# Two attentions of a transformer block: side work of TensorE cut into single products and pairs of transposes, spread over the key tiles

## The reference

```python
x = x + _L0_xattn_ref(_layernorm(x), ctx_1024, ctx_1024, mask, wq, bq, wk, bk, wv, bv, wo, bo)
x = x + _L0_ffn_ref(_layernorm(x), ...)    # 2 shared experts, top 2 of 8 routed experts
x = x + _L1_xattn_ref(_layernorm(x), ctx_1024, ctx_1024, key_padding_mask, Wq, bq, ...)
x = x + _L1_ffn_ref(_layernorm(x), theta, phi, theta_noise, phi_noise)

# both attentions
q, k, v = (split_heads(q), split_heads(k), split_heads(v))
score = jnp.einsum('bhqd,bhkd->bhqk', q, k) / jnp.sqrt(jnp.float32(HD))
alpha = jax.nn.softmax(score + mask, axis=-1)
context = jnp.einsum('bhqk,bhkd->bhqd', alpha, v)
return context.transpose(0, 2, 1, 3).reshape(b, -1, D) @ wo + bo

# _L1_ffn_ref
real = jnp.einsum('bti,io->bto', x, jnp.cos(theta + theta_noise))
imag = jnp.einsum('bti,io->bto', x, jnp.sin(phi + phi_noise))
return jnp.sqrt(real * real + imag * imag)
```

## Time and profile before

| | |
|---|---|
| median of 3 runs | 1262.23 us |
| the profiled execution | 1261.12 us |
| its span from first to last instruction | 1259.4 us |
| exponentials L925 on ACT | 800, 748.4 us busy |
| outputs L1834 on PE | 6400 instructions, 436.0 us busy |
| scores L1799 on PE | 6144 instructions, 316.4 us busy |
| query products L1627 | 96, 25.2 us busy |
| output projection L1861 | 128 instructions |
| wave products L1895 | 72, 19.7 us busy |

### The profile page before, as it was taken

The page is one execution under the profiler, slowest core; times in us unless marked ns, Lnnn a source line. Parts: engine busy times, 40 slices in busy tenths (PEclk is TensorE's granted clock), DMA queues, the critical chain, the costliest instruction groups (busy, mean ns, idle before and its releaser), DMA issues. The chain is left out here.

```text
span 1259.4 us, 43578 instructions
## 1 busy us (share of the span) xinstructions
PE 1164.9 (92%) x17850; PEld 581.9 (46%) x17850; DVE 720.3 (57%) x1697; ACT 1015.5 (81%) x1484; POOL 168.5 (13%) x204
## 2 busy tenths in 40 slices
PE   8888899899898999999999999988889999999897
PEld 5422232232222356667999998752222233232233
DVE  5325777767746577554666666662545444443447
ACT  3599999999999854443566666639999999999994
POOL 5111111011001030333000011032321000000000
PEclk9999999999999999999999999999999999999999
DMA  6235853643645333221343355133120010010002
GB/s 196 65 118 193 272 169 104 197 151 107 205 155 177 103 119 113 86 71 51 117 123 116 116 141 160 44 99 96 49 58 24 11 38 2 11 38 2 2 3 67
DMA packets 106305, 124.94 MB, mean 99 GB/s; under 512 B 25091, under 2 KB 89310, under 8 KB 106142
## 3 DMA queue, kind: packets, MB, share of 16 engines
q1 hardware_dynamic: 89088, 85.95, 22.1%
q0 software_dynamic: 9328, 29.37, 7.4%
q10 hardware_dynamic: 7726, 7.26, 1.9%
HBM read 70.27 MB, written 46.95 MB: 93 GB/s over the span
## 5 line engine op out<-in xcount | busy, mean ns | idle before, releaser
L925 ACT ACTIVATE prob<-banks 128x1024 f32<-128x1024 f32 x800 | 748.4, 1061 | 7.3 <-PE banks L1799 3.8
L1834 PE MATMUL banks<-prob,v 64*32 64x512 f32 x6400 | 436.0, 592 | 0.0
L1799 PE MATMUL banks<-zone,kst 52*32 52x512 f16 x6144 | 316.4, 383 | 65.7 <-ACT prob L925 58.2
L1799 PEld LDWEIGHTS banks<-zone,kst 52*32 52x32 f16 x6144 | 86.7, 89 | 444.0 <-ACT prob L925 429.5
L1834 PEld LDWEIGHTS banks<-prob,v 64*32 64x32 f32 x6400 | 117.4, 106 | 24.1 <-issue 2.2
L2503 PE MATMUL banks<-xsT_d,w 128*128 128x128 f16 x1776 | 123.6, 219 | 2.7 <-DMA w<-weight_parts 1.5
L2503 PEld LDWEIGHTS banks<-xsT_d,w 128*128 128x128 f16 x1776 | 108.6, 98 | 11.8 <-issue 8.8
L2514 PE MATMUL banks<-w,hh 128*128 128x256 f16 x592 | 107.0, 273 | 0.0
L2300 DVE TENSOR_TENSOR hl<-hid,hh 128x128 f16<-128x128 f32 x296 | 83.2, 291 | 30.9 <-ACT hh L2227 23.2
L2223 ACT ACTIVATE hid<-banks,b 128x128 f32<-128x128 f32 x222 | 74.5, 369 | 25.0 <-PE banks L2503 21.2
L2466 PE MATMUL banks<-w,hh 128*128 128x256 f16 x480 | 79.0, 273 | 2.1 <-DVE outb_d L2385 2.1
(11 more groups left out here) (302 smaller groups left out, 1367.2 us busy)
## 6 DMA issues: line engine op xcount, KB each, us to landing
weight_parts<-late SPq DMA_DIRECT2D x54, 256.0 KB, 3.9
w<-weight_parts POOLq DMA_DIRECT2D x24, 512.0 KB, 3.9
late<-in_L_ffn_W_r SPq DMA_DIRECT2D x43, 256.0 KB, 4.4
weight_parts<-more SPq DMA_DIRECT2D x26, 256.0 KB, 3.6
zone<-q_parts SPq DMA_DIRECT2D x180, 32.0 KB
slot_rows<-late POOLq DMA_DIRECT2D x14, 384.0 KB
more<-in_L_ffn_W_r SPq DMA_DIRECT2D x21, 256.0 KB, 4.2
xs_d<-slot_rows ACTq DMA_DIRECT2D x39, 128.0 KB, 2.1
```

Of the source, the lines that this page charges most:

```text
L925: nc.scalar.activation(prob[:, t % P_RING, 2 * (n % 2):2 * (n % 2) + 2, :], score[G % S_RING], ACT.Exp, scale=0.25).then_inc(exp_done, 1)
L1799: last = nc.tensor.matmul(score[G % S_RING][j:j + GROUP, a, :], kst[stack, 2 * q + n % 2, t * P + j:t * P + j + GROUP], qst[stack, u % Q_R ...
L1834: last = nc.tensor.matmul(outp[u % 2][GROUP * j:GROUP * (j + 1), a, :], v[rows, t, u % NQ, j, :], prob[rows, (u * KT + t) % P_RING, j if t ...
```

## The change

`plan` no longer takes tiles from a table. Every side work is cut into atoms: a single product of queries, output projection or waves, a pair of transposes, or one token tile's four logit products. Each group of atoms has a stretch of tiles `(t0, t1)` and is laid evenly over it, so a tile can get none, one or two atoms, which run one after the other at the tile's end. `turn_pair` replaces `turn_tokens` inside the units, `query`, `wave` and `logits` take an atom's index. The computed values, the waits in `begin`, VectorE's order and every other engine's order are the same. The tables of the last key's scores move by some tiles.

```diff
--- before.py
+++ after.py
@@ -97,11 +97,10 @@
-LAST_AT = ((4, 11, 10, 8), (5, 8, 5, 11))
+LAST_AT = ((4, 11, 11, 10), (5, 6, 6, 11))
...
-SIDES_AT = [((6, 7, 9, 10), (2, 3, 5, 6, 8, 9), (2, 4, 6, 8), (2, 4, 6)),
-            ((2, 4, 6, 7, 9, 10), (2, 4, 5, 7, 9, 10), (2, 4, 6, 8, 10, 11), (2, 4, 5, 7, 8, 10))]
-LATE_AT = ((), (7, 9), (2, 4, 6, 8), ())
...
+SIDE_PRODUCTS = DH * 3
...
@@ -1868,73 +1867,96 @@
                     last = nc.tensor.transpose(bank[:, i * P:(i + 1) * P], source[:, i, h * P:(h + 1) * P], g.ident[:])
                 last.then_inc(side_done, 1)
 
+            def turn_pair(name, c, h, k, source):
+                if k == 0:
+                    begin(name, c, h)
+                bank = side_bank(name, c, h)
+                for i in (2 * k, 2 * k + 1):
+                    last = nc.tensor.transpose(bank[:, i * P:(i + 1) * P], source[:, i, h * P:(h + 1) * P], g.ident[:])
+                if k == TPC // 2 - 1:
+                    last.then_inc(side_done, 1)
+
             def query(c, o, k):
                 if k == 0:
                     begin("query", c, o)
                     pe.wait_ge(side_free, at["turn", c, 1] + 1)
-                last = query_products(side_bank("query", c, o), o, (k,))
-                if k == DH - 1:
+                h, n = k // len(PRODUCTS), k % len(PRODUCTS)
+                a, b = PRODUCTS[n]
+                last = nc.tensor.matmul(side_bank("query", c, o), wqp[:, a, h, o * P:(o + 1) * P], xpT[:, b, h, :],
+                                        start=(k == 0), stop=(k == SIDE_PRODUCTS - 1))
+                if k == SIDE_PRODUCTS - 1:
                     last.then_inc(side_done, 1)
 
-            def logits(c):
-                bank = begin("logit", c, 0)
-                pe.wait_ge(cent_step, 4)
-                pe.wait_ge(side_free, at["xturn", c, 1] + 1)
-                for i in range(TPC):
+            def logits(c, tiles):
+                if tiles[0] == 0:
+                    begin("logit", c, 0)
+                    pe.wait_ge(cent_step, 4)
+                    pe.wait_ge(side_free, at["xturn", c, 1] + 1)
+                bank = side_bank("logit", c, 0)
+                for i in tiles:
                     for h in range(DH):
                         for a in range(PARTS):
                             last = nc.tensor.matmul(bank[:, i * 2 * E_R:(i + 1) * 2 * E_R], operands(c)[:, a, h, i * P:(i + 1) * P], centp[:, h, a, :],
                                                     start=(h == 0 and a == 0), stop=(h == DH - 1 and a == PARTS - 1))
-                last.then_inc(side_done, 1)
-
-            def wave(c, i, h):
-                if h == 0:
+                if tiles[-1] == TPC - 1:
+                    last.then_inc(side_done, 1)
+
+            def wave(c, i, k):
+                if k == 0:
                     begin("wave", c, i)
                     pe.wait_ge(side_free, at["xturn", c, 1] + 1)
-                for k, (a, b) in enumerate(PRODUCTS):
-                    last = nc.tensor.matmul(side_bank("wave", c, i), xpT[:, b, h, i * P:(i + 1) * P], g.wave[:, a, h, :],
-                                            start=(h == 0 and k == 0), stop=(h == DH - 1 and k == len(PRODUCTS) - 1))
-                if h == DH - 1:
+                h, n = k // len(PRODUCTS), k % len(PRODUCTS)
+                a, b = PRODUCTS[n]
+                last = nc.tensor.matmul(side_bank("wave", c, i), xpT[:, b, h, i * P:(i + 1) * P], g.wave[:, a, h, :],
+                                        start=(k == 0), stop=(k == SIDE_PRODUCTS - 1))
+                if k == SIDE_PRODUCTS - 1:
                     last.then_inc(side_done, 1)
 
             pe.wait_ge(shifts_loaded, 16 * 2 * NQ)
             def plan(c, q):
 
                 ahead, done = c + 1 < NC, c >= 1
-                turns = [("turn", c + 1, 0), ("turn", c + 1, 1)] if ahead else []
-                outs = [("out", c - 1, i, n, k) for i in range(DH) for n in range(2) for k in range(DH)] if done else []
-                asked = [("query", c + 1, o, k) for o in range(DH) for k in range(DH)] if ahead else []
-                back = [("xturn", c - 1, 0), ("xturn", c - 1, 1)] if done else []
-                waves = [("wave", c - 1, i, h) for i in range(TPC) for h in range(DH)] if done and not first else []
-                logit = [("logit", c - 1)] if done and first else []
-                if first:
-                    pieces = (outs[0:4], outs[4:8] + turns, asked[0:2] + back, asked[2:4] + logit)[q]
+                pairs = range(TPC // 2)
+                turns = [("turn", c + 1, h, k) for h in range(DH) for k in pairs] if ahead else []
+                outs = [[("out", c - 1, i, n, k) for n in range(2) for k in range(DH)] if done else [] for i in range(DH)]
+                asked = [[("query", c + 1, o, k) for k in range(SIDE_PRODUCTS)] if ahead else [] for o in range(DH)]
+                back = [("xturn", c - 1, h, k) for h in range(DH) for k in pairs] if done else []
+                waves = [[("wave", c - 1, i, k) for k in range(SIDE_PRODUCTS)] if done else [] for i in range(TPC)]
+                logit = [("logit", c - 1, i) for i in range(TPC)] if done else []
+                if first and done:
+                    groups = (((outs[0], 6, 10),), ((outs[1], 2, 6), (turns, 6, 10)),
+                              ((asked[0], 2, 8), (back, 8, 11)), ((asked[1], 2, 8), (logit, 8, 10)))[q]
+                elif first:
+                    groups = ((), ((turns, 7, 11),), ((asked[0], 2, 8),), ((asked[1], 2, 8),))[q]
+                elif done:
+                    groups = (((turns, 2, 5), (outs[0], 6, 10)), ((outs[1], 2, 6), (asked[0], 7, 13)),
+                              ((asked[1], 2, 6), (back, 7, 9), (waves[0], 10, 13)), ((sum(waves[1:], []), 2, 11),))[q]
                 else:
-                    pieces = (turns + outs[0:4], outs[4:8] + asked[0:2], asked[2:4] + back + waves[0:2], waves[2:8])[q]
-                times = SIDES_AT[layer][q]
-                if not first and not done:
-                    pieces, times = ([], turns, asked, [])[q], LATE_AT[q]
-                elif not done or q == 0 or (q == 2 and not first):
-                    times = times[len(times) - len(pieces):]
-                return {(LAST_AT if done else FIRST_LAST_AT)[layer][q]: ("last", c, q), **{t: piece for t, piece in zip(times, pieces)}}
+                    groups = ((), ((turns, 7, 11),), ((asked[0] + asked[1], 2, 10),), ())[q]
+                at_tile = {t: [] for t in range(KT)}
+                for atoms, t0, t1 in groups:
+                    for n, atom in enumerate(atoms):
+                        at_tile[t0 + n * (t1 - t0) // len(atoms)].append(atom)
+                at_tile[(LAST_AT if done else FIRST_LAST_AT)[layer][q]].append(("last", c, q))
+                return at_tile
 
             def side(name, c, *at_piece):
                 if name == "last":
                     last_scores(c, *at_piece)
                 if name == "turn":
-                    if at_piece[0] == 0:
+                    if at_piece == (0, 0):
                         pe.wait_ge(xn_ready, TPC * (c + 1))
-                    turn_tokens(name, c, at_piece[0], xn)
+                    turn_pair(name, c, *at_piece, xn)
                 if name == "out":
                     project_out(c, *at_piece)
                 if name == "query":
                     query(c, *at_piece)
                 if name == "xturn":
-                    if at_piece[0] == 0:
+                    if at_piece == (0, 0):
                         pe.wait_ge(on_ready, TPC * (c + 1))
-                    turn_tokens(name, c, at_piece[0], on)
+                    turn_pair(name, c, *at_piece, on)
                 if name == "logit":
-                    logits(c)
+                    logits(c, at_piece)
                 if name == "wave":
                     wave(c, *at_piece)
 
@@ -1951,8 +1973,8 @@
                         outputs((u * KT + t - 1) // KT, (t - 1) % KT)
                     if t < KT - 1 and G + 1 < UNITS * PAIRS:
                         scores(G + 1)
-                    if t in pieces:
-                        side(*pieces[t])
+                    for piece_of_work in pieces[t]:
+                        side(*piece_of_work)
             outputs(UNITS - 1, KT - 1)
 
             def hidden_ahead(a, b):
...
```

2 lines of the change are left out of this document (1 added, 1 removed).

## The result

The changed kernel takes 1271.39 us (median of five runs, 1269.51 to 1275.41) against 1262.23 us: a ratio of 1.0069 with the 95% interval 1.0054 to 1.0084. The forecast was 1263.4 us with a range of 1258.5 to 1269.5. The profiled execution took 1271.39 us, its span is 1269.6 us.

A forecast was written before the change was run, and what follows sets the result against it. The prediction took the attentions as a race between ACT's exponentials and PE, with a unit floor of about 23.0 us; its terms summed to +1.25 us, 1262.4 us profiled and a 1263.4 us median, range 1258.5 to 1269.5.

The forecast's parts named there:

- c=0 of the first attention: First attention, chunk 0: queries as single products on tiles 2 to 7 bring three units to 23.06 us each, -0.75 us.
- Rival 3: First attention, q=2, q=3: cuts waiting for loads delay the read-out, PE waits; about 1 us in eight units, 1271 us; chance 0.06.
- The waves: Second attention, q=3: six threes become nine twos, -0.15 us three times, -0.45; first wave on tiles 10 to 12 costs the same.
- the queries with their last product on tile 12: Second attention, c=1, 2, q=1: singles free on tiles 7 to 11, 0.2 us on 12, against 0.68 before; -1.0 us.
- the first chunk of the second attention: Second attention, c=0: four pieces of three become twelve products on eight tiles; -0.3 us with the turns.
- Output projection, +2.1 + 1.4: Units q=0 and q=1, both attentions: each gap lost between output products costs a 0.23 us credit; +2.1 and +1.4 us.
- Single products are free: A tile with one query product takes PE 1.74 us, leaving 0.08 us to spare against ACT's pace.
- rival 2: Tiles with pieces grow from 123 to 191; each break costs 0.23 us on the path, +15.6 us, 1278 us; chance 0.03.
- VectorE, +0.6 and +0.7: Late last scores in first attention, c=1, 2, 0.3 us each; late read-out before second attention's c=1 first wave, 0.7 us.
- Tile 12: Second attention: a single query product there was charged 0.2 us; the first wave reaching it was said to cost the same.

The follow-up runs named there:

- e1_c0_later: Changed kernel with the first attention's chunk 0 query products on tiles 5 to 9 (q=2) and 4 to 7 (q=3), not 2 to 7; 1269.97 us, ratio 1.0049.
- e2_one_cut_later: Changed kernel with one VectorE weight cut moved from the first attention's second unit to a unit of chunk 3; 1271.15 us, ratio 1.0063.
- e9_combined: Changed kernel with later chunk 0 queries, gaps between output products, waves as threes, second attention's transposes back as fours on tiles 6, 8; 1262.42 us, ratio 0.9999.
- e5_fewer_cuts: Changed kernel with 3, 4, 5 weight cuts in the first chunk's q=1, 2, 3, not 5, 6, 6; last chunk takes five over; 1268.14 us, ratio 1.0048.
- r_after: The changed kernel, word for word, run once more; 1276.30 us, ratio 1.0099 against the kernel before.
- e3_before_c0_early: Kernel before with only the first attention's chunk 0 query pieces of three moved to tiles 2 and 4; 1269.38 us, ratio 1.0046.
- e8_before_rows: Kernel before with only the gaps between the output products closed, in both attentions; 1268.02 us, ratio 1.0036.
- r_before: The kernel before, word for word, run once more for a second profile; 1263.18 us, ratio 1.0008.

## Why the prediction missed, step by step

**The failed step: c=0 of the first attention.** The forecast had "For c=0 three units take 69.95 us ... by three units of 23.06 us that gives -0.75 us". It was +5.8 us, so this term was 6.5 us off, of the 8.0 by which the median missed. There the queries were costed by their columns only, and PE's wait for the read-out was put at nothing; it was 4.06 us, and the unit grew by 5.2. The rule that `begin` wants `out_read` was known, and the lateness of VectorE was worked out, but only for c=1, from the earlier trace rows; chunk 0 has another order of cuts, and its queries were moved furthest, from tiles 6 and 8 to tile 2. The two VectorE rows of the kernel before, shown under the result, held the answer: the read-out ends at 106.90 + 0.69 = 107.6 us, 10.0 us after the unit's first exponential (97.6 us). In the changed kernel PE was through the score ahead of the first query product at 102.8 us, 6.4 us after that unit's first exponential: 3.6 us too early for a VectorE that stands as before. With a later tile (e1_c0_later) or three cuts ahead of the read-out (e2_one_cut_later) the unit was back at 23.0 us.

**Rival 3 was the right mechanism in the wrong place.** It named cuts that wait for loads, the read-out behind them and PE at its first piece, and gave 1271 us, which is the time that came; that the totals agree is luck. It spread the loss as 1 us over eight units. It was 5.2 and 0.9 us in two; in c=1 and c=2 PE waited on tile 2 only in q=3, 0.34 and 0.62 us, and against the unit of e9_combined (22.98 us) and without the late last scores 0.1 and 0.4 us of that stayed. Its 0.06 of chance rested on a lateness worked out for c=1.

**The rest of the sum came within 1 us, in part by luck.** The third unit of c=0's term, q=1, fell by 0.33 us. Without the three both attentions grew by 7.34 + 1.47 - 5.16 - 0.95 + 0.33 = 3.0 us; the terms other than c=0's give +1.25 + 0.75 = 2.0 us. The waves, and the queries with their last product on tile 12, missed by 1.2 and 0.6 us (below); the first chunk of the second attention (-0.9 us, of it 0.46 in its first unit, for -0.3) and the rest of its units q=2 (-0.6 us) made up for most of it.

- *Output projection, +2.1 + 1.4.* Units q=0 grew by 0.21 to 0.29 us. With q=1 the lost gaps come to 3.6 us, taking for q=1 the 0.25 and 0.44 us of c=3, which has no other change there. PE's rows of two such tiles answer to the earlier trace rows: 2.05 us from score to score, each time.

```profile
164.51 0.40 PE L1798 MATMUL banks<-zone,kst 52*32 52x512 f16 x8
164.84 0.70 PE L1860 MATMUL banks<-wo,late 128*128 128x256 f32 x2
...
166.56 0.40 PE L1798 MATMUL banks<-zone,kst 52*32 52x512 f16 x8
166.89 0.70 PE L1860 MATMUL banks<-wo,late 128*128 128x256 f32 x2
...
168.61 0.40 PE L1798 MATMUL banks<-zone,kst 52*32 52x512 f16 x8
```

- *Single products are free, rival 2 falls.* A query tile, first attention, c=1, q=2; 209.99 - 208.16 = 1.83 us, ACT's own pace; so the 1.74 us that PE alone was said to need can't be read here. The unit q=2 is 0.18 us shorter, where 0.28 were said.

```profile
208.16 0.40 PE L1798 MATMUL banks<-zone,kst 52*32 52x512 f16 x8
208.49 0.39 PE L1885 MATMUL banks<-xpT,wqp 128*128 128x512 f16 x1
...
209.99 0.40 PE L1798 MATMUL banks<-zone,kst 52*32 52x512 f16 x8
```

The score ahead of the product is followed after 0.33 us, as in the earlier trace rows, so the change of array form is still paid, in the tile's spare time. The Trainium skill (TensorEngine Tiling (Array Packing), Key Properties) states "Mode switching requires drain"; these rows agree that a change costs (0.33 us against 0.21), and it decided nothing here.

- *VectorE, +0.6 and +0.7.* c=1 and c=2 lost 0.26 and 0.38 us to late last scores (0.3 each was said): so much later than before come the first three exponentials of their q=3, and in e5_fewer_cuts, with the same tiles and other cuts, it is 0.02 and 0.14 us. In the second attention PE's first wave product waited as said (0.54 us, expected 0.7), and c=1, q=3 grew by 0.87 us where c=2, which has no such wait, grew by 0.26:

```profile
1034.29 0.60 PE L1910 MATMUL banks<-wave,xpT 128*128 128x512 f16 x2 [0.54 <-DVE late L1240]
```

- *Tile 12, under-sized.* A piece there was put at 0.2 us and "costs the same" for the first wave. It costs 0.5 us for one product. In c=1 and 2 of the second attention q=1 fell by 0.24 us, which is 0.68 less for the threes and 0.44 more for the gaps, as said; but the first three exponentials of q=2, behind the product on tile 12, come 0.64 us late (against ACT's pace of 0.90 us each) where they came 0.14 us late before. So these queries brought 2 x (0.5 - 0.68) = -0.36 and not -1.0 us; the rest of q=2 gave 0.29 us back in each. For two wave products on tile 12 the same three exponentials are 0.90 us late and not 0.54. So the waves were not -0.45 but +0.75 us (0.26, 0.26 and 0.23, without c=1's wait).

**The medians follow the two attentions.** After is longer by 7.3 + 1.5 = 8.8 us there and by 9.2 us in the median. Over the other rows of the table the sum of the two attentions, against that of the kernel before, differs from the median's difference by 2.2 us or less but for r_after (9.0 against 13.8 us, mostly ahead of the first attention) and e9_combined (-2.5 against -0.1).

## What to carry to other kernels

Before a piece is moved earlier, ask for each engine that it waits for, and for each chunk apart, when that engine is there now; a stall that costs nothing today shows in the trace as an idle engine in front of work that nobody wants yet. An engine that works in a fixed order, with loads in its list, can turn a shift into waits one or two units further on, in both directions: too early meets the read-out, too late meets the last scores. Where PE and ACT are this close, a free slot is worth more between costly pieces than behind them, and the piece to avoid is the one at the unit's end.

## What the runs showed of the hardware

The granted clock fell behind the wait. These are stretches of the changed kernel around it (start:end, length, busy us of each engine, granted clock, share of DMA, GB/s):

```profile
103.00:107.00 4.00, 0.13 (x1) 0.10 (x1) 3.55 (x6) 1.01 (x2) 0.70 (x1) 1.00 1.03 370
107.00:111.00 4.00, 4.00 (x50) 1.08 (x57) 3.03 (x5) 2.08 (x3) 0.00 (x0) 0.57 0.31 100
```

PE did next to nothing for 4 us, then ran at 0.57 of full speed on the mean, mostly at 1.2 GHz: its output products take 1.95 us there and 1.04 us at 2.4 GHz. So ACT, after its 3.70 us of idle time, waited another 1.11 us, and 4.06 us of PE's waiting became 5.2 us of unit. In r_after, with the same wait, the clock stayed down longer, and the unit grew by 5.5 us:

```profile
108.00:117.00 9.00, 5.35 (x66) 1.25 (x66) 6.56 (x10) 3.73 (x4) 0.48 (x1) 0.62 0.57 198
```

Unsettled is the way between the attentions: 429.4 and 428.7 us in the two profiles of the kernel before, 431.0 to 433.5 in all others, of which e3_before_c0_early and e8_before_rows have the same instructions there. In e3_before_c0_early 1.7 us of it lies in a stretch at half the clock among the experts. In every other profile 1.3 to 2.1 us more than in before come in the last 44 us before the second attention. The granted clock of the last 5 us is 1.00 in both profiles of before and 0.66 to 0.77 in all eleven others. First r_before, then the changed kernel:

```profile
848.00:853.00 5.00, 2.64 (x15) 1.36 (x14) 1.13 (x6) 1.23 (x6) 1.69 (x3) 1.00 0.48 142
```

```profile
857.00:862.00 5.00, 4.20 (x28) 1.73 (x28) 0.00 (x0) 1.70 (x9) 1.43 (x2) 0.66 0.44 132
```

The Trainium skill (TensorE: Matmul & The Clock Gate, Part 1) says that the chip's look at TensorE's activity is free-running and does not start with the kernel, so the same code may meet it differently; that fits e3 and e8, but two profiles of before that agree speak for more than chance, and no run here decides it. In the table it is 2.3 us of the changed kernel's profile, beside 8.8 us in the two attentions. Since most medians follow the two attentions alone to about 2 us, it can be a small part of the 9.2 us at most; how much of it is in the medians, no run separates.
